# A decoder layer on one core: values reordered by DMA through a scratch, q one step ahead, new order on every engine

## The reference, cut to what matters

```python
# attention: the 16 heads of ONE token attend to each other
q, k, v = x @ Wq.T + bq, x @ Wk.T + bk, x @ Wv.T + bv     # each (B, S, 16, 32)
q, k = rope(q), rope(k)
att = softmax(einsum('bshd,bstd->bsht', q, k) / sqrt(32))
x1 = layernorm(x + swap(einsum('bsht,bstd->bshd', att, v)) @ Wo.T + bo)
# cross attention: a gated linear attention (mLSTM) over the tokens, queries x1, keys and values ctx
D = exp(log_D - max_log_D); C = q @ k.T / sqrt(32) * D
h = C / max(|sum C|, exp(-max_log_D)) @ v                 # per head, then normalised per head
x2 = layernorm(x1 + h * ln_scale)
# feed forward: 8 small experts, the best one by a score is taken
y = layernorm(x2 + expert(x2))
```

## Time and profile before

| | |
|---|---|
| median of 3 runs | 1725.87 us (1724.93 to 1728.69) |
| the profiled execution | 1729.01 us, span 1727.5 us |
| mean granted TensorE clock | 0.976 of full |
| busy TensorE, VectorE, ScalarE, GpSimd | 90%, 80%, 49%, 54% |

### The profile page before, as it was taken

The page is one execution under the profiler, slowest core; times in us unless marked ns, Lnnn a source line. Parts: engine busy times, 40 slices in busy tenths (PEclk is TensorE's granted clock), DMA queues, the critical chain, the costliest instruction groups (busy, mean ns, idle before and its releaser), DMA issues.

```text
span 1727.5 us, 67777 instructions
## 1 busy us (share of the span) xinstructions
PE 1550.4 (90%) x27491; PEld 1222.5 (71%) x27619; DVE 1378.1 (80%) x3401; ACT 854.6 (49%) x2385; POOL 931.3 (54%) x1232
## 2 busy tenths in 40 slices
PE   0788899899999999999999999999999999999964
PEld 0566777677777777777777777777777777777752
DVE  4355788788888888888888888888888888888875
ACT  2044544545554555455545545554555455545552
POOL 1024555546655665566556555655565556556653
PEclk9899999999999999999999999999999999999985
DMA  4021222222222222222222222222222322222210
GB/s 153 25 76 63 77 93 76 77 95 73 83 87 98 73 82 88 96 75 81 90 88 82 80 91 79 91 75 96 74 94 76 98 73 87 84 98 73 79 57 31
DMA packets 53829, 141.14 MB, mean 82 GB/s; under 512 B 8767, under 2 KB 10431, under 8 KB 45578
## 3 DMA queue, kind: packets, MB, share of 16 engines
q1 hardware_dynamic: 53770, 140.31, 24.1%
HBM read 122.98 MB, written 17.30 MB: 81 GB/s over the span
## 4 chain that ended last, share of the span: by engine, by line
PE 80%; issue 7%; ACT 6%; DVE 4%; POOL 1%; SPq 1%; DMA 0%; POOLq 0%; ACTq 0%; DVEq 0%
PE bank L358 16%; PE bank L359 13%; PE bank L361 13%; PE bank L350 6%; PE quad L422 5%; PE quad L409 4%; PE quad L468 4%; PE bank L480 4%; PE bank L503 4%; PE bank L448 4%; PE quad L490 3%; DVE VT L862 2%; ACT Hs L649 2%; ACT VG L586 2%; ACT cT L602 1%
## 5 line engine op out<-in xcount | busy, mean ns | idle before, releaser
L746 POOL TENSOR_TENSOR ex<-ex,w_rec 128x512 f32<-128x512 f32 x64 | 67.0, 1047 | 595.0 <-DVE w_rec L902 595.0
L642 ACT ACTIVATE Dx<-Mb,a_col 128x128 f32<-128x128 f32 x1024 | 311.6, 390 | 3.4 <-DMA Mb<-m_rows 3.4
L766 POOL TENSOR_TENSOR h_rs<-h_ve,half_neg 128x16 f32<-128x16 f32 x64 | 187.7, 2933 | 40.0 <-DVE h_ve L979 40.0
L612 ACT ACTIVATE x1T<-bank 128x512 f32<-128x512 f32 x64 | 38.2, 597 | 308.9 <-PE bank L350 308.9
L961 DVE SCALAR_TENSOR_TENSOR Dx<-quad,Dx 128x512 f32<-128x512 f32 x256 | 158.9, 682 | 12.2 <-PE quad L468 4.6
L751 POOL TENSOR_SCALAR_AFFINE_SELECT Dx<-Dx 128x512 f32<-128x512 f32 x256 | 160.2, 639 | 3.5 <-ACT Dx L642 3.5
L780 POOL TENSOR_TENSOR rs<-ve,half_neg 128x1 f32<-128x1 f32 x192 | 104.9, 546 | 69.4 <-DVE ve L923 67.2
L358 PE MATMUL bank<-wq_high,x_high 128*128 128x512 f32 x256 | 117.3, 458 | 3.6
L358 PE MATMUL bank<-wv_high,x_high 128*128 128x512 f32 x256 | 113.1, 442 | 1.6 <-issue 1.6
L358 PE MATMUL bank<-wk_high,x_high 128*128 128x512 f32 x256 | 113.0, 441 | 0.0
L422 PE MATMUL quad<-PT,VG 32*32 32x32 f32 x8192 | 83.7, 202 | 29.1 <-ACT VG L586 18.4
(11 more groups left out here) (166 smaller groups left out, 4375.9 us busy)
## 6 DMA issues: line engine op xcount, KB each, us to landing
Mb<-m_rows SPq DMA_DIRECT2D x64, 1024.0 KB, 4.7
xb<-in_x SPq DMA_DIRECT2D x256, 64.0 KB
xr<-in_x SPq DMA_DIRECT2D x64, 256.0 KB, 3.9
cb<-in_ctx SPq DMA_DIRECT2D x64, 256.0 KB, 2.6
out_dram<-yo SPq DMA_DIRECT2D x64, 256.0 KB, 3.9
Dx<-in_wq SPq DMA_DIRECT2D x4, 256.0 KB, 4.5
Dx<-in_wk SPq DMA_DIRECT2D x4, 256.0 KB, 5.4
Mb<-in_wv SPq DMA_DIRECT2D x4, 256.0 KB, 6.0
```

The lines of the kernel that those rows point to most:

```text
L642: last = go(Dx[t.parity()][:, j, n, :], Mb[t.parity()][:, h, :], ACT.Exp, bias=a_col[t.parity()][:, h:h + 1], scale=-1.0)
L766: tt(h_rs[:], h_ve[:], half_neg[:], ALU.pow).then_inc(s.hrs_sb, 1)
```

## The change

The transposes of v on TensorE go, and with them VectorE's turning of v and ScalarE's copy of VG. v is copied once by ScalarE from bank 7 to SBUF as it is (`v_sb`), stored to a scratch in DRAM and loaded back in the order that the sums over keys want, 16 runs of 128 bytes for each partition. For the heads to fit, k is turned with another pattern of writing. v is now computed for the tile `a`, after the sums over keys of `b`; q for `a` moves ahead, to v's former place, and the transposes of x move to the head of TensorE's step. On VectorE the turning of q stands between the sum and the transposition of the exponentials, the scans move behind the subtraction, `r_stats` behind the reciprocal, `x_gate` ahead of `r_y`. On GpSimd c1 moves ahead of the power. Where parts only pass from the end of a list to the head of it (ScalarE's m_gs, m_softplus, x_LT, m_HT, a_exp), the order of the engine is the same, and they take the next tile's letter. 62 instead of 27 small matmuls warm TensorE. The patterns `pairs` of the mask of scores follow k's.

```diff
-WARM = 27
+WARM = 62
-        VT = sb("VT", [P, E])
-        VG = sb("VG", [P, CH, P])
+        v_sb = sb("v_sb", [P, E])
+        VG = sb("VG", [P, 4, CH, D])
+        v_dram = nc.dram_tensor("v_rows", (2, P, E), F32, kind="Internal").ap()
...
 SP
+            def store_v(t):
+                sp.wait_ge(s.v_sb, upto(t))
+                sp.dma_start(v_dram[t.parity()], v_sb[:]).then_inc(s.v_out, 16)
+
+            def load_VG(t):
+                sp.wait_ge(s.v_out, stored(t.older(-1)))
+                sp.wait_ge(s.O_ps, upto(t, 1))
+                source = v_dram[t.parity()].rearrange("(u m) (h d) -> (m h) u d", m=8, d=D)
+                sp.dma_start(VG[:].rearrange("p w c d -> p (w c) d"), source).then_inc(s.v_in[t.parity()], 16)
...
                 if n2.real():
                     sp.wait_ge(s.xT_ps, upto(n2, 2))
                     load_x(n2)
+                if a.real():
+                    store_v(a)
                 if n1.real():
                     sp.wait_ge(s.r1_sb, upto(n1, 2))
                     load_res(n1)
                 if f.real():
                     store(f)
+                if a.real():
+                    load_VG(a)
                 if c.real():
                     spread_M(c)
...
 TensorE
             def p_xT(t):
...
-                    pe.wait_ge(s.cT_sb, upto(t, 1))
-                    pe.wait_ge(s.Hs_sb, upto(t, 4))
+                    pe.wait_ge(s.x1T_sb, upto(t, 2))
...
             def p_v(t):
-                pe.wait_ge(s.fn1_sb, upto(t, 4))
-                bias(4, 2)
-                product(4, x_high, x_low, 2, False).then_inc(s.v_ps, 1)
-
-            def p_VG(t):
-                pe.wait_ge(s.VT_sb, upto(t))
-                transposes(bank[4], VT).then_inc(s.VG_ps, 1)
+                pe.wait_ge(s.acol_sb, upto(t, 2))
+                bias(7, 2)
+                product(7, x_high, x_low, 2, False).then_inc(s.v_ps, 1)
...
             def a_O(t):
-                pe.wait_ge(s.VG_sb, upto(t))
+                pe.wait_ge(s.v_in[t.parity()], landed(t, 1))
...
             def m_gate(t):
+                pe.wait_ge(s.v_sb, upto(t, -1))
...
             def x_Y(t):
                 pe.wait_ge(s.LT_sb, upto(t))
+                pe.wait_ge(s.Hs_sb, upto(t, -3))
...
 TensorE, step
+                    p_xT(a)
                     m_gate(c)
                     a_S(b)
                     m_HT(d)
-                    p_v(b)
+                    p_q(a)
                     m_H(d)
                     m_cT(b)
                     m_aT(c)
                     x_Y(g)
-                    p_VG(b)
-                    p_xT(a)
                     a_O(b)
-                    p_q(a)
+                    p_v(a)
                     x_x2T(e)
...
 ScalarE
-            def p_VG(t):
-                act.wait_ge(s.VG_ps, upto(t))
-                go(chunks(VG), bank[4][:], ACT.Copy).then_inc(s.VG_sb, 1)
+            def p_v(t):
+                act.wait_ge(s.v_ps, upto(t))
+                if t.regs is not None or t.k >= 1:
+                    act.wait_ge(s.v_out, stored(t))
+                go(v_sb[:], bank[7][:], ACT.Copy).then_inc(s.v_sb, 1)
...
 ScalarE, step
+                    p_xT(a)
+                    m_gs(c)
+                    m_softplus(c)
+                    x_LT(g)
+                    m_HT(d)
+                    a_exp(b)
                     m_Hs(d)
...
                     r_sq(d)
                     x_exp(f)
-                    p_VG(b)
                     m_acol(c)
-                    p_xT(a)
                     a_O(b)
                     m_Dx(c, 2)
                     m_Dx(c, 0)
                     m_Dx(c, 1)
                     x_x2T(e)
+                    p_v(a)
                     m_Dx(c, 3)
                     x_yo(g)
                     m_x1T(b)
-                    m_gs(b)
-                    m_softplus(b)
-                    x_LT(f)
-                    m_HT(c)
-                    a_exp(a)
...
 GpSimd, step
                     x_score(e)
                     r_nn(c)
+                    m_c1(b)
                     r_pow(c)
                     rsqrt(f, ve3, rs3, s.ve3_sb, s.rs3_sb, s.yo_sb)
                     x_nm(f)
                     r_y2(c)
-                    m_c1(b)
                     m_mask(b, 2)
...
 VectorE
-            def turn(dst, b):
-                return nc.vector.transpose(dst[:].rearrange("p (g h n) -> p h g n", h=H, n=2), bank[b][:])
+            def turn(dst, b, order):
+                return nc.vector.transpose(dst[:].rearrange(order + " -> p h g n", h=H, n=2), bank[b][:])
...
-                turn(QT, 4).then_inc(s.QT_sb, 1)
+                turn(QT, 4, "p (g h n)").then_inc(s.QT_sb, 1)
...
-                turn(KT, 6).then_inc(s.KT_sb, 1)
+                turn(KT, 6, "p (g n h)").then_inc(s.KT_sb, 1)
-
-            def p_VT(t):
-                dve.wait_ge(s.v_ps, upto(t))
-                turn(VT, 4).then_inc(s.VT_sb, 1)
...
 VectorE, step
+                    p_low(a)
+                    m_gsum(c)
                     a_max(b)
                     a_sub(b)
-                    x_choose(f)
+                    m_scan(c)
                     a_sum(b)
                     a_rec(b)
+                    r_stats(e)
+                    p_QT(a)
+                    a_PT(b)
+                    x_choose(f)
                     r_norm(d)
-                    p_VT(b)
-                    a_PT(b)
+                    x_y3(g)
                     r_var(d)
-                    x_y3(g)
-                    p_low(a)
                     r_x2(e)
+                    a_low(b)
                     x_stats(g)
-                    a_low(b)
+                    x_gate(f)
                     r_y(d)
-                    x_gate(f)
-                    p_QT(a)
                     a_r1(b)
                     a_stats(b)
                     a_x1(b)
                     p_KT(a)
                     m_C(c, j) for j in (1, 3, 0, 2)
                     x_shift(e)
-                    m_gsum(b)
-                    r_stats(d)
-                    m_scan(b)
```

More of the change, by code:

```diff
@@ L226, in bass_decoder @@
             shift_set pads_set high_set low_set center_set mean_set""".split()
-        each = """xT_ps xhigh_sb xlow_sb q_ps k_ps v_ps QT_sb KT_sb VT_sb VG_ps VG_sb xres_sb
+        each = """xT_ps xhigh_sb xlow_sb q_ps k_ps v_ps QT_sb KT_sb v_sb xres_sb
             S_ps max_sb sub_sb ex_sb sum_sb rec_sb exn_sb PT_sb
@@ L237, in bass_decoder @@
         four = "Dx_sb Dm_sb C_sb".split()
-        two = "x_in c_in r_in mb_in".split()
-        semaphores = {n: sem(n) for n in once + each + ["y_out", "m_out"]}
+        two = "x_in c_in r_in mb_in v_in".split()
+        semaphores = {n: sem(n) for n in once + each + ["y_out", "m_out", "v_out"]}
         semaphores |= {n: [sem(f"{n}{j}") for j in range(4)] for n in four}
@@ L277, in steps @@
                 dma = {(n, k): eng.snap(u * (16 * n) + 16 * n * k) for n in (1, 4) for k in range(-1, 2)}
-                dma |= {("out", k): eng.snap(u * 32 + 16 * k) for k in range(-LAGS, 2)}
+                dma |= {("out", k): eng.snap(u * 32 + 16 * k) for k in range(-LAGS, 3)}
                 for k in range(2):
@@ L415, in a_O @@
                 pe.wait_ge(s.PT_sb, upto(t))
-                pe.wait_ge(s.VG_sb, upto(t))
-                edge(pe, t, (s.Hs_sb, 3), (s.sub_sb, 0), *[(s.C_sb[j], 2) for j in range(4)])
+                pe.wait_ge(s.v_in[t.parity()], landed(t, 1))
+                edge(pe, t, (s.Hs_sb, 2), (s.sub_sb, 0), *[(s.C_sb[j], 2) for j in range(4)])
                 for v in range(4):
@@ L421, in a_O @@
                             rows = slice(32 * c, 32 * c + 32)
-                            last = mm(quad[32 * w:32 * w + 32, c, 32 * v:32 * v + 32], VG[rows, v, 32 * w:32 * w + 32],
+                            last = mm(quad[32 * w:32 * w + 32, c, 32 * v:32 * v + 32], VG[rows, w, v, :],
                                       PT[rows, w, v, :], start=True, stop=True, skip_group_check=True,
@@ L694, in step @@
                 b, c, d, e, f, g = [a.older(n) for n in range(1, 7)]
+                if a.real():
+                    p_xT(a)
+                if c.real():
+                    m_gs(c)
+                    m_softplus(c)
+                if g.real():
+                    x_LT(g)
+                if d.real():
+                    m_HT(d)
+                if b.real():
+                    a_exp(b)
                 if d.real():
@@ L1066, in pairs @@
             def pairs(t, rows, n):
-                return t[rows, :].rearrange("p (g n) -> p g n", n=2)[:, :, n]
+                if t is pair_l:
+                    return t[rows, :].rearrange("p (g h n) -> p g h n", h=H, n=2)[:, :, :, n]
+                return t[rows, :].rearrange("p (g n h) -> p g n h", h=H, n=2)[:, :, n, :]
             nc.vector.memset(pairs(pair_l, slice(0, P), 1), 1.0).then_inc(s.center_set, 1)
```

40 lines of the change are left out of this document (15 added, 25 removed).

## The result

| | before | after |
|---|---|---|
| median | 1725.40 us (1724.74 to 1728.69, 4 runs) | 1708.15 us (1706.93 to 1709.52, 4 runs) |
| span of the profiled execution | 1727.5 us | 1705.2 us |
| TensorE, VectorE, GpSimd busy | 90%, 80%, 54% | 89%, 75%, 56% |

The ratio after to before is 0.9896, 95% interval [0.9879, 0.9914]: the changed kernel is 1.0% faster. The forecast was 1727 us; 1708 lies in its range, outside the likeliest case's own range.

The account below looks back on a forecast made before the run. The loop from row maxima through VectorE and GpSimd to x1 and back was to bind: 19.1 + 5.8 = 24.9 us a step against 24.81, +5 us; first and last steps -4, warming +3; forecast 1727 us, range 1672 to 1773.

Parts of the forecast that it names:

- the likeliest case: Whole kernel: the forecast itself, 1727 us, a tie with before; own range 1714 to 1740 us, chance 0.42.
- 1.55 us a step: TensorE: what the values' four transposes and two waits cost it; forecast to be lost again in two new waits.
- D: Rival, SP's load of VG: takes 16 us and landing, sums over keys wait 2 to 4 us a step; 1850 us and more, chance 0.04.
- E: Rival: TensorE alone binds, a step of 23.26 us, 1634 us in all; chance 0.04.
- B: Rival, VectorE: h_ve and x2 run beside GpSimd's c1 instead of waiting for it; 1676 us, chance 0.25.
- the 0.61 us between x1's end and its transposes: TensorE before: the only slack VectorE's path has; a larger gain per step needs a shorter way between maxima.
- Part 2: VectorE and GpSimd, start of the row maxima (M) to x1: 19.1 us in the new order, 2.0 later than before.
- Part 3: From x1 to the next row maxima: 5.8 us, with TensorE's path and the path through k's turning and C tied.
- 0.70 as for pairs of words: VectorE's turning of k: writing single words 64 B apart takes 0.70 us, no longer than pairs.
- Four steps at most of the 1.55: First and last steps: tiles are missing, VectorE has less to do, TensorE's gain shows; about -4 us.
- +3 with a bound of 3.9: Start of the kernel: 35 more warming matmuls cost up to 3.9 us, taken as +3 us.
- C's 0.7 us a step: Rival, VectorE's turning of k: the new pattern is slower, bounded by another 0.70 us; step 25.6, 1773 us, chance 0.25.

Follow-up runs that it names:

- novw72: Kernel before without the values' transposes on TensorE and ScalarE's copy of VG (VG a constant), 72 warming matmuls: 1733.8 us, 1.0054 against before.
- ktpairs: Changed kernel with k turned in pairs of words as before, loaded values keeping the new order (they meet other heads' weights): 1690.2 us, 0.9792 against before.
- c1late: Changed kernel with c1 back at its old place on GpSimd, behind y2: 1743.6 us, 1.0103 against before.
- c1idle: Changed kernel with c1 moved into GpSimd's idle stretch and the load of ctx behind the values' load on SP: 1688.7 us, 0.9788 against before.
- ryfirst: Changed kernel with r_y ahead of the gate on VectorE, as before the change: 1737.5 us, 1.0072 against before.

## Why the prediction was wrong, point by point

**Right: the mechanism of the steady step.** Of TensorE's 1.55 us a step only 0.28 were gained; the rest turned into waits ahead of QK, for C, for x1 and for Hs. The wait ahead of QK is 0.6 us, not the "over 1 us" of the forecast. The loop from M through VectorE and GpSimd to x1, and through k's turning, C and the scores to the next M, sets the step: moving one GpSimd copy changes it both ways, 24.9, 24.5, 24.2. c1 holds VectorE, the gate ahead of r_y is short (1.56, forecast 1.57), y2 follows r_y at once, and the load of VG is hidden (3.9 us to landing where 3.4 and 4 were taken). Rivals D and E are out by this, and B, h_ve and x2 running beside c1: x2 starts at M + 9.15, not at 8.6. novw72 goes against E in the old order as well, and against a reading of the prediction: the 0.61 us between x1's end and its transposes are no slack that TensorE could have taken, for with less work on TensorE the step stays.

**Wrong: the size of the step**, 24.53 against 24.9; this is the step of the prediction that failed. By the terms of Part 2: x2 at M + 9.15 against 9.5, as c1 came 0.2 earlier and x2 followed its end at once, with h_ve stretched instead of pushed back; x2 to r_y 3.81 against 3.87; y2 to rsqrt 4.30 against 4.4. Together that is 0.5 less. Part 3 gives 0.1 back (5.89 against 5.8). Each term is within 0.35 us, but over 60 steps 0.4 us are 24, more than the whole effect. The prediction had seen it ("the hand sum has rounded every wait up") and taken 3 us off for it where some 20 were due. Its own sum of 1733 us for the profiled execution stands against 1706.9: 20 of the 26 us are the steady step, 10 the first steps, and start and tail give 3 back.

**Luck: the range.** 1708 lies in it because the range reaches down to B, 1727 less 0.85 x 60 = 1676. B did not happen: x2 starts at c1's end (M + 9.13, by the medians). Nor does the power set r_y: it is done at M + 12.48, 0.5 ahead of r_y, which waits for the gate.

**Wrong within Part 3: two errors that nearly cancel.** The turning of k "0.70 as for pairs of words" took 1.07; from its start to that of C it is 0.93 instead of 0.63 (ktpairs). And the 1.58 us from x1 to C, read from before, hold a wait: there C started 0.07 after the end of QK and 0.82 after k's turning began.

```profile
1044.57 1.17 PE L468 MATMUL quad<-x1T,cT 32*128 32x128 f32 x32
```

With QK early, x1 to C takes 1.39 in ktpairs and 1.69 in the kernel after. So the path through C, which the prediction held for tied with TensorE's, sets S in both, and of the two errors, 0.30 too little and 0.19 too much, 0.11 are left.

**Wrong: the first steps.** "Four steps at most of the 1.55", -4, measured -13.9 over eleven. What makes it is open. It is not the transposes alone, since novw72 without them gains 0.4 there, and the kernels of the new order with 42 packets spread from 273.3 (ktpairs) to 283.9 (c1late). The start cost +5.6, against +3 with a bound of 3.9: the first M comes at 70.91 with 27 warming matmuls and at 73.28 with 62, so 2.4 are the warming and 3.3 the new order, which the prediction put at nothing. No run shows the +3 itself; it was the author's estimate.

**Two sums of the prediction** don't come out, without weight for the forecast: C's 0.7 us a step over 60 steps is 42, not 46 (1769), and E's 93 us are counted from the step of before, 24.81 less 23.26, but taken off the forecast, whose step is 24.9.

**The warming** was costed as time alone. Its greater effect was not looked for: with 27 this kernel takes 1963 us, 255 more. No row of before could show it, and the prediction held no rival of this kind.

## What to carry to other kernels

When the forecast difference (here 0.09 us a step) is no larger than the rounding of one term, a hand sum can say which mechanism binds, but not the sign; give each rounding its direction and multiply it by the number of steps before choosing the forecast. An instruction of GpSimd that holds VectorE belongs where GpSimd is idle and VectorE works on what it doesn't hold (here C, which reads PSUM: 2.46 us beside c1 in c1idle, 2.46 without it in the kernel after): the same copy was worth -19 or +35 us by its place. After any edit to a long loop on TensorE look at the number of instruction packets first; if it has risen, shift the code and measure again before judging the edit.

## What the runs showed of the hardware that was not expected

- The place of a loop's code: 42 or 276 packets of instructions, 1708 or 1963 us, for 35 small matmuls more or less in front of it. In between (105 and 87 packets) single steps grow to 34.5 and 35.4 us, and the times of one kernel spread over 1.4 and 3.4%. Why these two fall in between was not tried.
- VectorE's 32x32 transposition of 128x512 takes 0.70 us writing pairs of words and 1.07 writing single words 64 B apart.
- The power on GpSimd takes 3.24 us in every variant of the kernel after and 2.93 in before and in its two variants; in the kernel after it is done before r_y is reached, and its cause was not tried.
- A small operation of VectorE can be recorded as lasting to the end of GpSimd's instruction: h_ve 0.73 us instead of 0.17, to 1020.18, where c1 ends at 1020.15. Three operations of the gate in the kernel before, and the mask beside the last of them:

```profile
1038.46 0.16 DVE L1029 TENSOR_REDUCE g_max<-gate 128x1 f32<-128x8 f32 x1
1038.65 0.87 DVE L1031 SCALAR_TENSOR_TENSOR g_key<-gate,g_max,xrow_sb 128x8 f32<-128x8 f32 x1
...
1039.75 0.76 DVE L1039 TENSOR_SCALAR L<-g_key,g_kmax,g_max 128x8 f32<-128x8 f32 x1
1040.54 0.61 DVE L1041 TENSOR_TENSOR L<-fz,L 128x64 f32<-128x64 f32 x1
...
1040.44 0.64 POOL L751 TENSOR_SCALAR_AFFINE_SELECT Dx<-Dx 128x512 f32<-128x512 f32 x1
```

g_key and the two L end at 1039.52, 1040.51 and 1041.15; y2 and c1 end at 1039.50 and 1040.48, the mask at 1041.08. In the tail, where GpSimd runs only an rsqrt and nm (0.54 and 0.27 us), the three take 0.23, 0.29 and 0.23. All three go from SBUF to SBUF, with two tensors or with scalars per row, as do h_ve and, in ryfirst, the last L (1.29, to 1016.30, where r2 ends at 1016.21); g_max, a reduction, takes 0.16 beside y2 as in the tail. The whole gate takes 1.56 ahead of y2 in the kernel after and 3.5 beside y2, a mask and r2 in ryfirst. Not every instruction of GpSimd holds VectorE: in the kernel after the gate's g_key, of the form that takes 0.94 beside y2 in ryfirst, takes 0.23 at 1023.06, inside the power (1020.26 to 1023.50). Why some do and some don't was not shown.
